# Two copies of the masks: a short arm for pairs without failed rows, a second copy inside the long body

## The reference, cut to what matters

```python
def _top_p_attention(X, W1, W2, W3):
    q = X @ W1.T @ W2.T
    k = X @ W3.T
    probs = softmax(q @ k.T)
    idx = argsort(-probs)
    sp = take_along_axis(probs, idx)
    cs = cumsum(sp)
    keep_sorted = cs - sp < 0.9
    A = probs * mask            # the kept ones, back in their places
    return A / maximum(A.sum(-1), 1e-12)

R = S + eye(N); R = R / R.sum(-1)
for n in range(2):
    A = _top_p_attention(Xa, W1, W2, W3)
    Xf = R @ Xf
    Xa = A @ Xa
    Z = Z + Xf @ U1[n].T + Xa @ U2[n].T
h = X + Z            # then two layer norms, with X added between them
```

## Time and profile before

| | |
|---|---|
| median of 3 runs | 1642.84 us (1642.64 to 1643.18) |
| the profiled execution | 1643.45 us, of which the span is 1641.7 us |
| mean granted clock of TensorE | 0.878 |
| busy: PE, DVE, ACT, POOL | 76%, 86%, 54%, 11% of the span |
| DMA | 96.40 MB, mean 59 GB/s |
| instructions of DVE | 7395 |

### The profile page before, as it was taken

The page is one execution under the profiler, slowest core; times in us unless marked ns, Lnnn a source line. Parts: engine busy times, 40 slices in busy tenths (PEclk is TensorE's granted clock), DMA queues, the critical chain, the costliest instruction groups (busy, mean ns, idle before and its releaser), DMA issues.

```text
span 1641.7 us, 29435 instructions
## 1 busy us (share of the span) xinstructions
PE 1243.3 (76%) x9162; PEld 1058.4 (64%) x9162; DVE 1411.7 (86%) x7395; ACT 893.5 (54%) x1685; POOL 173.0 (11%) x357
## 2 busy tenths in 40 slices
PE   8888888888888989898988957539672909366870
PEld 4666765667676978787877856537562808365870
DVE  4788878888885989898899988989898989988984
ACT  5676667766666555555566543515552525335435
POOL 0200000000010331322212100001000100000000
PEclk9999999999999989898989988869785959778885
DMA  5100000000021431222305130303030211203101
GB/s 178 43 2 1 2 1 2 2 1 2 2 82 45 152 141 63 106 92 78 132 37 168 43 125 1 126 1 125 2 126 1 85 42 43 84 1 126 43 1 42
DMA packets 16588, 96.40 MB, mean 59 GB/s; under 512 B 1251, under 2 KB 8930, under 8 KB 9730
## 3 DMA queue, kind: packets, MB, share of 16 engines
q1 hardware_dynamic: 16384, 94.14, 16.3%
HBM read 92.43 MB, written 1.70 MB: 57 GB/s over the span
## 4 chain that ended last, share of the span: by engine, by line
DVE 68%; PE 17%; issue 7%; ACT 5%; DVEq 1%; DMA 0%; SPq 0%; ACTq 0%
DVE cand L745 18%; DVE junkC L788 17%; PE bank L546 8%; DVE E L1119 6%; DVE E L1121 6%; PE bank L525 3%; PE bank L486 3%; DVE slots L843 2%; ACT E L620 2%; DVE sub L944 2%; DVE junkS L788 2%; DVE st L796 1%; DVE st L797 1%; DVE st L798 1%; DVEq L924 1%
## 5 line engine op out<-in xcount | busy, mean ns | idle before, releaser
L647 ACT ACTIVATE blkT<-bank 128x512 f32<-128x512 f32 (+1 forms) x728 | 411.9, 566 | 500.2 <-PE bank L525 496.0
L745 DVE MAX8 cand<-E 128x8 f32<-128x32 f32 (+1 forms) x3172 | 409.7, 187 | 16.3 <-ACT E L597 15.5
L546 PEld LDWEIGHTS bank<-X,blkT 128*128 128x128 f32 x2704 | 337.0, 195 | 132.6 <-issue 67.3
L546 PE MATMUL bank<-X,blkT 128*128 128x128 f32 (+1 forms) x2704 | 380.9, 284 | 48.7 <-ACT blkT L647 47.5
L525 PE MATMUL bank<-ident,E 128*128 128x128 f32 x1144 | 196.0, 300 | 281.3 <-DVE E L1121 281.3
L525 PEld LDWEIGHTS bank<-ident,E 128*128 128x128 f32 x1144 | 153.6, 157 | 286.0 <-DVE E L1121 284.6
L788 DVE SCALAR_TENSOR_TENSOR junkC<-cand,st 128x208 f32<-128x208 f32 (+1 forms) x416 | 301.9, 762 | 3.7
L525 PE MATMUL bank<-ident,S 128*128 128x128 f32 x1560 | 240.5, 274 | 7.0 <-DVE S L1121 6.1
L486 PE MATMUL bank<-kT,Q 64*128 64x512 f32 (+1 forms) x728 | 196.7, 615 | 7.8 <-ACT E L597 6.9
L546 PE MATMUL bank<-YA,blkT 128*128 128x128 f32 x1352 | 194.0, 289 | 1.1 <-ACT blkT L647 1.1
L597 ACT ACTIVATE E<-bank 128x512 f32<-128x512 f32 (+1 forms) x308 | 157.8, 565 | 64.8 <-PE bank L486 64.0
(11 more groups left out here) (203 smaller groups left out, 1159.3 us busy)
## 6 DMA issues: line engine op xcount, KB each, us to landing
S<-in_adj_dram SPq DMA_DIRECT2D x50, 1663.5 KB, 6.9
S<-in_adj_dram SPq DMA_DIRECT2D x2, 1455.6 KB, 8.2
X<-in_x_dram SPq DMA_DIRECT2D x6, 256.0 KB, 4.1
out_dram<-H SPq DMA_DIRECT2D x2, 768.0 KB
S<-in_adj_dram SPq DMA_DIRECT2D x2, 194.9 KB, 9.5
u_in<-in_L_gnn_U_dram SPq DMA_DIRECT2D x4, 64.0 KB, 9.5
w_in<-in_L_gnn_W_dram SPq DMA_DIRECT2D x2, 32.0 KB, 2.1
X<-in_x_dram SPq DMA_DIRECT2D x1, 64.0 KB
```

The source lines that it names most:

```text
L546: m = pe.matmul(bank[int(u.acc)][:, 0:width], blkT[:, slot, b * P:(b + 1) * P], rhs[:, j, 0:width], start=(j == 0), stop=(j == NT - 1))
L647: act.activation(blkT[:, slot, 0:w], BLK[early][slot][:, 0:w], ACT.Copy).then_inc(blk_done, 1)
L745: v.max(cand[:, par, xx, 8 * r:8 * r + 8], E[where_e[self.s, self.p]][:, xx, r * w:min((r + 1) * w, N)]).then_inc(s_max, 1)
```

## The change

The flag is read earlier: behind 8 of the remaining maxima DVE's sequencer waits for the last step of `reduce_flags` (which is now posted without a wait of its own), behind 8 more it loads the flag, and then come the other maxima and the negation. The masks are a function `settle`. It stands in a short arm that is gone through if the flag is 0, and again in the long body: behind `level` if no row is left, and behind `by_tile`. The wait on sums_ready, which stood before the masks, comes behind them. All lines from 50 on move down by one, those behind the search by more: L1105 and L1109 stay, L1119 becomes L1115, L1121 becomes L1117, L1124 becomes L1145.

```diff
--- before.py
+++ after.py
@@ -47,6 +47,7 @@
     AIM = 20.0
     K_FULL = 42
     QUARTERS = 4
+    READ_BEHIND = 8
     QW = NP // QUARTERS
     HALF = [NP // 2, N - NP // 2]
 
@@ -918,7 +919,7 @@
                         link(ins)
                     else:
                         link.post(ins)
-                link(v.tensor_reduce(flag_i[:, :], flag_4[:, :], AX.X, ALU.max))
+                link.post(v.tensor_reduce(flag_i[:, :], flag_4[:, :], AX.X, ALU.max))
 
             def load_flag(n):
                 return dve.value_load(flag_i[n:n + 1, 0:1], min_val=0, max_val=3)
@@ -1078,7 +1079,15 @@
                         runs.step(2 * BANK // RUN[1])
                     dve.wait_ge(e_ready, gp + 1)
                     fill = 0 if (s, p) == (0, NPAIR - 1) else 1 if s == 0 or p == 0 else 0
-                    search(Chain(s_search, runs, fill, 8 if s else 0), s, par)
+                    link = Chain(s_search, runs, fill, 8 if s else 0)
+                    search(link, s, par)
+
+                    if p + 1 < NPAIR:
+                        runs.step(READ_BEHIND)
+                    dve.wait_ge(s_search, link.n)
+                    if p + 1 < NPAIR:
+                        runs.step(READ_BEHIND)
+                    code = load_flag(0)
                     if p + 1 < NPAIR:
                         runs.finish()
 
@@ -1089,37 +1098,49 @@
                             with dve.If(load_flag(1 + xx) > 0):
                                 drop_ties(e, xx)
 
-                    with dve.If(load_flag(0) > 0):
+                    def settle():
+
+                        link = Chain(s_tie)
+                        if s:
+                            link(v.tensor_tensor(gone[:, :, :, :], rank[:, :, :, :],
+                                                 excess[:, :, :].rearrange("p x (n a) -> p x n a", a=1).to_broadcast([P, 2, MATCH, 8]),
+                                                 ALU.is_le))
+                            flat = "p x n k -> p x (n k)"
+                            link(v.tensor_tensor(gone[:, :, :, :].rearrange(flat), gone[:, :, :, :].rearrange(flat),
+                                                 wide(two(TSTAR), 8 * MATCH), ALU.mult))
+                        for xx in range(2):
+                            if s:
+                                for k in range(MATCH):
+                                    back = e[:, xx, k * MW:(k + 1) * MW][:, ::-1]
+                                    link.post(v.match_replace(back, gone[:, xx, k, :], back, 0.0))
+                                dve.wait_ge(s_tie, link.n)
+                            v.scalar_tensor_tensor(out=e[:, xx, :], in0=e[:, xx, :], scalar=one(TSTAR, xx), in1=e[:, xx, :],
+                                                   op0=ALU.is_ge, op1=ALU.mult, accum_out=one(SUM, xx)).then_inc(a_ready, 1)
+
+
+                    with dve.If(code < 1):
+                        settle()
+                    with dve.If(code > 0):
                         if s:
                             for xx in range(2):
                                 with dve.If(load_flag(1 + xx) > 1):
                                     level(e, xx)
-                            reduce_flags(Chain(s_slow))
-                            with dve.If(load_flag(0) > 0):
+                            link = Chain(s_slow)
+                            reduce_flags(link)
+                            dve.wait_ge(s_slow, link.n)
+                            left = load_flag(0)
+                            with dve.If(left < 1):
+                                settle()
+                            with dve.If(left > 0):
                                 by_tile()
+                                settle()
                         else:
                             by_tile()
-
-                    if s:
-                        link = Chain(s_tie)
-                        link(v.tensor_tensor(gone[:, :, :, :], rank[:, :, :, :],
-                                             excess[:, :, :].rearrange("p x (n a) -> p x n a", a=1).to_broadcast([P, 2, MATCH, 8]),
-                                             ALU.is_le))
-                        flat = "p x n k -> p x (n k)"
-                        link(v.tensor_tensor(gone[:, :, :, :].rearrange(flat), gone[:, :, :, :].rearrange(flat),
-                                             wide(two(TSTAR), 8 * MATCH), ALU.mult))
+                            settle()
                     link = Chain(s_tie)
                     if gp >= 2:
                         q = gp - 2
                         dve.wait_ge(sums_ready, a_unit[q // NPAIR, 2 * (q % NPAIR) + 1].k + 1)
-                    for xx in range(2):
-                        if s:
-                            for k in range(MATCH):
-                                back = e[:, xx, k * MW:(k + 1) * MW][:, ::-1]
-                                link.post(v.match_replace(back, gone[:, xx, k, :], back, 0.0))
-                            dve.wait_ge(s_tie, link.n)
-                        v.scalar_tensor_tensor(out=e[:, xx, :], in0=e[:, xx, :], scalar=one(TSTAR, xx), in1=e[:, xx, :],
-                                               op0=ALU.is_ge, op1=ALU.mult, accum_out=one(SUM, xx)).then_inc(a_ready, 1)
                     dve.wait_ge(a_ready, 2 * gp + 2)
                     link(v.tensor_tensor(two(SUM), two(SUM), two(LEAST), ALU.max))
                     v.reciprocal(a_inv[:, par, :], two(SUM)).then_inc(inv_ready, 1)
```

## The result

| | before | after |
|---|---|---|
| median of 4 runs | 1642.74 us (1640.70 to 1643.18) | 1614.32 us (1612.99 to 1615.77) |
| ratio | | 0.983, 95% interval 0.9813 to 0.9847 |
| the profiled execution | 1643.45 us | 1615.12 us (span 1613.3) |
| mean granted clock of TensorE | 0.878 | 0.887 |
| busy: PE, DVE, ACT, POOL | 76, 86, 54, 11% | 77, 87, 56, 17% |

The kernel is 28.4 us faster, by the medians. The forecast was 1619.7 us, 23.1 less than before: the right side and the right mechanism, 5.4 us short of the gain.

A forecast was written before the change was run, and what follows sets the result against it. DVE alone was taken to set the pace from pair 18 on, PE and ACT in step 1. The terms -20.8 - 4.7 + 1.4 + 1.0 = -23.1 us gave 1619.7 us, range 1606 to 1634.

The forecast's parts named there:

- pairs 18 to 25, gaps before the masks: DVE, step 2: gaps of 24.1 us shrink to 5.3 us, saving 18.8 us.
- pair 22, stall behind the jump: DVE, between the masks' second and third operation: the 2.02 us stall goes with straight-line masks, saving 2.0 us.
- failed pairs, head: Saved load (0.6) offsets near jump over the short arm (0.5): 0; +2.3 us in each of 5 pairs if missed.
- second stalls: Further stalls following the far jump behind the masks: +1.0 us over eight pairs, between 0 and 6.
- pairs 13 to 17: DVE could reach pair 18's search 16.4 us earlier; ACT's exponentials allow 4.7: -4.7 us, between -3.5 and -16.4.
- step 1, the clock: PE's idle time comes in one piece, lowering its clock: +1.4 us; the 27 us saved before masks gain 0.
- 0.85 us behind failed bodies: Gap before the masks where the load stays exposed: load 0.65, branch 0.1, clear and start 0.1.
- The cover: Behind the masks, the 2.9 us far jump is hidden by the 3.69 us last product; 2.9 us per pair if not.
- rival C: Cover of the far jump behind the masks fails: slower, 1645.6 to 1649 us; chance 0.08.
- Rival D: Cover holds, but near jumps over the short arm miss and stalls follow: 16.5 us less gain, 1636; chance 0.10.
- Rival A: All of step 2 gained; ACT and PE in bodies 13 to 17 give way too: 1608.0 us; chance 0.12.

The follow-up runs named there:

- masks once: Changed kernel with the early flag read, but the masks once, behind the body, with the jump in front of them: 1638.2 us, ratio 0.9979.
- load late: Changed kernel with the flag loaded behind the last maximum and the negation, as before; short arm kept: 1620.14 us, ratio 0.9875.
- Without the cover: Changed kernel, but DVE's sequencer waits for the masks' last product before the far jump: 1638.45 us, ratio 0.9983.
- pairs 14 to 17 in the old form: Changed kernel with late flag read and masks once behind the body in pairs 14 to 17 only: 1623.3 us, ratio 0.9884.
- twelve traces: Profiles of the study's kernels and variants; DVE's instructions from pair 18 to the last product take 616.3 to 619.2 us in them.
- ACT freed: Changed kernel with three units of R, not four, in bodies 13 to 17 and four, not three, in 18 to 22: 1599.97 us, ratio 0.9741.
- step 1 old: Changed kernel with flag, branch and masks of step 1 as before, step 2 as after: 1614.64 us, ratio 0.9839.
- nine traces named above: Five profiles with after's step 1 (head of pair 13 at mean 524.6 us) and four with before's (mean 523.3 us).
- small loads: Changed kernel with adjacency loads from the seventh on cut to their first 64 columns: 1615.94 us, timed once.
- a schedule that was worthless before the change: Kernel before, with three units of R in bodies 13 to 17 and four in 18 to 22: 1644.49 us, ratio 1.0013.

## Why the prediction was right, and where its sizes were off

By the prediction's own steps, forecast and then measured, in us:

| step | forecast | measured |
|---|---|---|
| pairs 18 to 25, gaps before the masks | -18.8 | -19.0 |
| pair 22, stall behind the jump | -2.0 | -2.0 |
| failed pairs, head | 0 | -2.5 |
| second stalls | +1.0 | 0 |
| not forecast: L913 (-0.3), DVE's instructions themselves and the gaps under 0.2 us (-2.0) | 0 | -2.3 |
| pairs 13 to 17 | -4.7 | -4.8 |
| step 1, the clock | +1.4 | +2.3 |
| sum | -23.1 | -28.3 |

**Gaps.** Shown by both halves of the change: with the masks once they are back (23.0 us), with the load late each is 0.6 longer. The 0.85 us behind failed bodies were met to the hundredth.

**The cover.** The far jump of 2.9 us lies beside a product of 3.69. Without the cover 24 of the 28 us are lost, so rival C named the step on which the whole gain rests, and its price per jump (2.9 us; measured 3.2 to 3.45 with the start) nearly right. Its condition did not hold here.

**Failed heads, the first mis-sized step.** The prediction charged a taken jump over the short arm with 0.5 us, the price of the near jumps in step 1, and the saved load with 0.6. The load's share was right; the jump takes less. In pair 18, sequencer, the branch of the short arm and the branch at its target:

```profile
L1121 DVEq COMPARE_BRANCH  x1: 67/67/67, 959.6 to 959.6; - x1
...
L1123 DVEq COMPARE_BRANCH  x1: 50/50/50, 959.9 to 959.9; - x1
```

0.22 us from one to the other. So there is a third level below the two that the rows of before showed: a jump over the short arm is dearer than going straight on (0.09) and cheaper than 0.5. -2.5 us over five pairs. Rival D had expected these to miss: not one did.

**Second stalls, the second mis-sized step.** They were put at +1.0, between 0 and 6. None came in pairs 18 to 25. One came without the cover (1.36 us, pair 22), one with the masks once (1.7) and one with pairs 14 to 17 in the old form (2.3): they exist, and what decides whether one comes was not tried. That none came here is luck as far as the prediction goes.

**Not forecast.** L913 waits 0.3 us less. The masks of one pair are one Chain now, so the clear between the second and the third operation is gone (0.1 us in seven pairs), but the small gaps of the stretch together are only 0.1 us less. The other 1.9 us are DVE's instructions themselves (616.3 in place of 618.3 us). After is the lowest of the twelve traces there, so these 1.9 us are within what executions differ by and can't be credited to the change.

**Pairs 13 to 17.** The step argued from slack and not from busy shares: DVE is 16.4 us faster and gets 4.7. Measured -4.75, and the head of pair 18 stands 0.23 us behind ACT's exponentials, as all heads of step 1 do. With ACT freed the stretch gives 13.7 us more. Rival A, which expected PE's earlier start to carry ACT along, is refuted.

**Step 1.** No gain, as said. The price in clock was taken from one body that ran at 0.95 in place of 1.00. In the run there were three stretches of 6.8 in place of 3.4 us, one of them ahead of any mask, and one at 289 us where none was; two traces with the old step 1 (step 1 old, masks once) have that one too. Over the nine traces named above the price is 1.2 us and not 2.3, close to the 1.4 forecast, but the reason given for it was borne out in one body only (115 us). That the size came out is partly luck.

## What to carry to other kernels

A taken branch costs 0.5 us when its target is at hand and some 3 us when it is not, and the length of the body doesn't tell which: over the same body of step 1 the kernel before had seven short jumps and six long ones. It costs nothing when it is placed behind an instruction that runs longer than the fetch: a short copy of the common path, jumping far only behind its last long operation, buys that. Before crediting a saved gap, read how much slack the other loop has at the next meeting point; past it nothing is gained until that loop is relieved as well, and a schedule that was worthless before the change is then worth testing again.

## What the runs showed of the hardware

**A jump has three prices, and a fourth beside a load.** On DVE's sequencer: 0.22 us over the short arm, 0.50 to 0.57 where the target was at hand, 2.7 to 3.2 where it was not (2.3 in pair 1 of after), and 4.3 to 5.6 where a load of 1.7 MB had been issued 2.2 to 3.7 us before. The Trainium skill says that a taken branch out of the current two pages forces a DMA fetch of the target page ("Runtime: NRT & Kernel Launch", section "Instruction fetch mechanics"). The small loads agree with that: 2.76 to 2.77 us in place of 5.57, 4.28 and 4.87. It makes the time of a jump depend on what SP issued a few microseconds earlier.

**POOL waits for a product, and the product for POOL.** POOL's additions at L437 (L436 before) went from a mean of 571 to 1926 ns. They used to start in the gaps before the masks, at 171.62 us in pair 3; now they fall beside the products. POOL after:

```profile
173.76 3.60 POOL L437 TENSOR_TENSOR H<-hy,H 128x128 f32<-128x128 f32 x1 [16.16 <-ACT hy L684]
```

DVE after:

```profile
173.37 3.69 DVE L1117 SCALAR_TENSOR_TENSOR E<-E,st 128x3328 f32<-128x3328 f32 x1
...
176.98 3.87 DVE L1117 SCALAR_TENSOR_TENSOR E<-E,st 128x3328 f32<-128x3328 f32 x1
```

The addition, 0.45 us otherwise, starts within the first product and ends at 177.36, 0.3 us behind it; the second product is 0.18 us longer than its usual 3.69. The Trainium skill has DVE and GpSimd share a port pair that one of them holds for a whole instruction while the other blocks ("SBUF — State Buffer", section "Terms"), and this trace agrees. POOL had time to spare here, so the rise of its busy time from 173 to 270 us costs nothing that shows; a kernel bound by POOL would pay it.
